# A decoder layer on one core: two more groups of unused products between the first transpositions, later landings in the planner's table, and a new order

## What is computed

```python
x = x + _L0_attn_ref(_layernorm(x, axis=-1), Wq, bq, Wk, bk, Wv, bv, Wo, bo)      # causal, with alibi bias
x = x + _L0_xattn_ref(_layernorm(x, axis=-1), ctx_2048, mask_BxS2_bk0)            # ctx is both key and value
x = x + _L0_ffn_ref(_layernorm(x, axis=-1), up_kernel, up_bias, down_kernel, down_bias)
# ffn: gelu(h @ fp4(up_kernel) + up_bias) @ fp4(down_kernel) + down_bias
# fp4: blocks of 32 rows share a power-of-two scale, codes 0, .5, 1, 1.5, 2, 3, 4, 6
```

## Time and profile before

| | us |
|---|---|
| median of 3 runs | 136.51 |
| lowest and highest | 135.77, 137.06 |
| the profiled execution | 137.31 |
| its span, first to last instruction | 135.5 |
| TensorE busy | 119.1 (88%) |
| VectorE busy | 108.1 (80%) |
| ScalarE busy | 84.3 (62%) |
| GpSimd busy | 75.5 (56%) |

### The profile page before, as it was taken

The page is one execution under the profiler, slowest core; times in us unless marked ns, Lnnn a source line. Parts: engine busy times, 40 slices in busy tenths (PEclk is TensorE's granted clock), DMA queues, the critical chain, the costliest instruction groups (busy, mean ns, idle before and its releaser), DMA issues. The chain is left out here.

```text
span 135.5 us, 3237 instructions
## 1 busy us (share of the span) xinstructions
PE 119.1 (88%) x1060; PEld 87.1 (64%) x1060; DVE 108.1 (80%) x253; ACT 84.3 (62%) x180; POOL 75.5 (56%) x140
## 2 busy tenths in 40 slices
PE   0939899999999999979999999764998989999990
PEld 0829346745557785657786766633556878999990
DVE  5382995899998799988989999969977696854632
ACT  2130479349888768856877787757568588545520
POOL 7844400145959833754661667891745979544430
PEclk9995999999999999999999999999599999999999
DMA  4999605999700000000000000000000002020112
GB/s 125 288 356 381 220 6 151 374 344 384 171 0 5 5 0 0 5 0 0 0 7 0 0 5 0 0 0 2 5 0 0 0 0 85 0 77 0 47 35 77
DMA packets 8880, 10.69 MB, mean 79 GB/s; under 512 B 1665, under 2 KB 7937, under 8 KB 8737
## 3 DMA queue, kind: packets, MB, share of 16 engines
q1 hardware_dynamic: 7776, 9.64, 21.2%
q10 hardware_dynamic: 1088, 0.86, 2.1%
HBM read 9.45 MB, written 1.05 MB: 77 GB/s over the span
## 5 line engine op out<-in xcount | busy, mean ns | idle before, releaser
L623 POOL TENSOR_TENSOR s_sb<-s_sb,s_max 128x512 f32<-128x512 f32 x16 | 16.8, 1052 | 24.9 <-DVE s_max L837 24.9
L957 DVE TENSOR_TENSOR h_lo<-h_sb,h_hi 128x256 fp32r<-128x256 f32 x32 | 15.6, 495 | 8.3 <-POOL h_hi L612 8.3
L1132 PE MATMUL bank<-xn_T,w_up_q 128*128 128x256 f16 x128 | 20.1, 291 | 1.4 <-ACT h_sb L753 1.0
L753 ACT ACTIVATE h_sb<-bank,bias_cols 128x256 f32<-128x256 f32 x32 | 14.9, 474 | 9.9 <-PE bank L1132 8.9
L612 POOL CAST h_hi<-h_sb 128x256 fp32r<-128x256 f32 x32 | 14.0, 444 | 11.7 <-ACT h_sb L753 11.7
L1148 PE MATMUL bank<-w_down_q,h_hi 128*128 128x256 f32 x64 | 18.6, 317 | 0.0
L585 POOL TENSOR_TENSOR rstd<-var_eps,minus_half 128x1 f32<-128x1 f32 x24 | 16.0, 666 | 2.0
L1148 PE MATMUL bank<-w_down_q,h_lo 128*128 128x256 f32 x64 | 16.3, 281 | 0.0
L581 POOL TENSOR_SCALAR var_eps<-mean_var 128x1 f32<-128x1 f32 x24 | 8.3, 345 | 14.4 <-DVE mean_var L786 13.6
L653 ACT ACTIVATE xn_T<-bank 128x256 f32<-128x256 f32 x16 | 6.1, 383 | 15.8 <-PE bank L990 15.6
L1003 PE MATMUL bank<-xn_T,w_T 128*128 128x512 f32 x32 | 14.6, 600 | 0.5 <-issue 0.5
(11 more groups left out here) (88 smaller groups left out, 260.8 us busy)
## 6 DMA issues: line engine op xcount, KB each, us to landing
raw_T<-in_W_up_T_dram SPq DMA_DIRECT2D x1, 1024.0 KB, 9.1
raw<-in_W_up_dram SPq DMA_DIRECT2D x1, 1024.0 KB, 11.8
raw_T<-in_W_down_T_dram SPq DMA_DIRECT2D x1, 1024.0 KB, 5.6
raw<-in_W_down_dram SPq DMA_DIRECT2D x1, 1024.0 KB, 8.1
ctx_T<-in_ctx_by_feature_dram SPq DMA_DIRECT2D x1, 1024.0 KB, 10.3
ctx_sb<-in_ctx_dram SPq DMA_DIRECT2D x1, 1024.0 KB, 13.0
out_dram<-x_sb SPq DMA_DIRECT2D x8, 128.0 KB, 1.7
x_sb<-in_x_dram SPq DMA_DIRECT2D x4, 128.0 KB, 3.9
```

What stands on the lines that cost most here:

```text
L623: pool.tensor_tensor(tile, tile, s_max[:, u % S_RING, :].unsqueeze(2).broadcast_to([P, HC, S]), ALU.subtract).then_inc(centred, 1)
L753: act.activation(h_sb[:, i % GELU_RING, :], bank[i % 2][:, 0:GN], ACT.Gelu_apprx_tanh, bias=bias_cols[:, BUP + f:BUP + f + 1], scale=1.0 / ...
L957: dve.tensor_tensor(h_lo[:, i % H_RING, :], h_sb[:, i % GELU_RING, :], h_hi[:, i % H_RING, :].bitcast(F32), ALU.subtract).then_inc(split_r ...
L1132: last = pe.matmul(dst[:, 0:GN], w_up_q[:, c, f * P:(f + 1) * P], xn_T16[:, g * GT:(g + 1) * GT, at16:at16 + P], start=(k == 0), stop=(k = ...
```

## The change

The seven unused products stay where they are. After the first transposition three more are put into TensorE's list, and after the second three more again; each transposition of the first three tiles comes after its group. In the table the third tile's landing is planned 1.1 us later and the fourth's right behind it; the loads themselves are issued as before. The planned length of the query and key weights' load is 0.2 us shorter. All weights of the planner are replaced, and so the order of every queue may be another. The banks of three stages are read from tables, with the same values as before.

```diff
-WARM = 7
+WARM = (7, 3, 3)
...
-        add("turn", (n, t), "pe", 0.22, [("norm", (n, t))] + ([("warm", ())] if n == LN1 and t == 0 else []), [ln_bank(n, t)], last)
+        add("turn", (n, t), "pe", 0.22, [("norm", (n, t))] + ([("warm", (t,))] if n == LN1 and t < len(WARM) else []), [ln_bank(n, t)], last)
...
-    loads = (("load_x", (0,), 2.1), ("load_x", (1,), 0.6), ("load_v", (), 0.5), ("load_x", (2,), 0.8),
-             ("load_x", (3,), 1.0), ("load_biases", (), 0.1), ("load_qk", (), 2.2), ("load_x", (HALF,), 0.5),
+    loads = (("load_x", (0,), 2.1), ("load_x", (1,), 0.6), ("load_v", (), 0.5), ("load_x", (2,), 1.9),
+             ("load_x", (3,), 0.1), ("load_biases", (), 0.1), ("load_qk", (), 2.0), ("load_x", (HALF,), 0.5),
...
-    add("warm", (), "pe", 1.49, [("load_x", (0,))])
+    for i in range(len(WARM)):
+        add("warm", (i,), "pe", 0.22 * WARM[i], [("turn", (LN1, i - 1))] if i else [("load_x", (0,))])
...
-        add("prob_T", (u,), "pe", 0.49, [("exp", (u,))], [2 + u % 2], ("prob_copy", (u,)))
+        add("prob_T", (u,), "pe", 0.49, [("exp", (u,))], [prob_bank(u)], ("prob_copy", (u,)))
...
 URGENCY = {
...
-    "attn_turn": 354, "quant": 142, "normalise": 100, "pv": 59, "binade": 55, "prob_T": 49, "x_table": 48,
+    "normalise": 149, "quant": 142, "x_scores": 124, "load_row_biases": 74, "v2_zero2": 51, "k_rest": 47,
...
-    "rstd": -5, "x2": -8, "scale_copy": -9, "spread_copy": -11, "x_prob_copy": -13, "q_inverse": -13,
-    "norm": -14, "v2_zero2": -15, "reload": -16, "q_step": -17, "load_qk": -18, "down": -18, "x_prob_T": -20,
...
-    "q_out": -43, "turn": -56, "scale_T": -65, "exp": -89, "x_read": -93, "v": -171,
+    "rows_copy": -38, "v": -38, "load_v": -39, "centre": -42, "rstd": -47, "x_prob_T": -49, "q_exponent": -58,
+    "x_exp": -58, "q_clip": -64, "spread_copy": -65,
...
 DRIFT = {
...
-    "binade": -6.4, "x_scale": -6.8, "norm": -7.6, "q": -8.0, "x2": -8.8, "k_rest": -9.6, "v_even": -10.4,
-    "x_prob_copy": -14.8, "q_cut": -19.2, "v_move": -24.0, "q_divide": -24.0, "scale_copy": -34.0,
-    "q_out": -36.8, "q_inverse": -140.8,
+    "v2_zero": 48.0, "scale_copy": 42.6, "binade": 40.0, "x_prob_T": 30.0, "low": 17.2, "v_copy": 12.0,
...
+    "max": -4.0, "x1": -4.4, "amax": -4.8, "load_x": -13.4, "k": -20.8, "v_move": -24.0, "q_round": -24.0,
+    "q_step": -57.6, "q_inverse": -302.4,
...
 PATIENCE = {
-    "act": 0.34, "pe": 0.12, "dve": 0.1, "pool": 0.0,
+    "pool": 0.38, "pe": 0.1, "act": 0.0, "dve": 0.0,
 }
...
                 if stage == "warm":
-                    for i in range(WARM):
+                    for i in range(WARM[at[0]]):
                         pe.matmul(bank[7][:, 0:P], ident, ident, start=True, stop=True)
...
+PROB_BANKS = (2, 3)
+UP_BANKS = ((0, 1), (0, 1), (0, 1), (0, 1))
+DOWN_BANKS = (2, 3, 2, 3)
```

More of the change, by code:

```diff
@@ L208, in stages @@
             add("split", (i,), "dve", 0.35, [("round", (i,))] + reused)
-            banks = [2 + g % 2] if f == 0 else []
+            banks = [down_bank(g)] if f == 0 else []
             add("down", (i,), "pe", 0.56, [("split", (i,)), ("q_out", (DOWN, 1))], banks, ("final", (tiles[-1],)))
@@ new lines @@
+    "prob_T": 2, "x_table": 2, "warm": 1, "q_cut": -2, "spread": -3, "q_add": -4, "q_out": -5, "load_ctx": -8,
+    "q": -10, "load_qk": -12, "add_bo": -13, "down": -13, "add_down": -15, "scale_copy": -15, "load_rows": -16,
+    "round": -19, "x_read": -19, "x_fill": -21, "load_o": -21, "q_divide": -21, "x_prob_copy": -21,
+    "store": -23, "k_flat": -25, "qk_bias": -26, "exp": -27, "load_alibi": -30, "scale_T": -33, "valid": -38,
+    "rows_copy": -38, "v": -38, "load_v": -39, "centre": -42, "rstd": -47, "x_prob_T": -49, "q_exponent": -58,
@@ L257 @@
+    "q": 4.0, "turn_copy": 3.8, "v_spread": 3.2, "x_scale": 3.2, "norm": 2.3, "spread_copy": 2.0,
+    "x_prob_copy": 1.2, "scores": 0.8, "exp": 0.2, "add": -0.4, "prob_T": -0.4, "split": -0.8, "centre": -1.2,
+    "normalise": -1.4, "attn_turn": -1.4, "x2": -1.6, "down": -2.1, "stats": -2.6, "warm": -3.3, "v_odd": -4.0,
+    "max": -4.0, "x1": -4.4, "amax": -4.8, "load_x": -13.4, "k": -20.8, "v_move": -24.0, "q_round": -24.0,
+    "q_step": -57.6, "q_inverse": -302.4,
 }
 PATIENCE = {
-    "act": 0.34, "pe": 0.12, "dve": 0.1, "pool": 0.0,
+    "pool": 0.38, "pe": 0.1, "act": 0.0, "dve": 0.0,
@@ L698, in _ @@
                         act.wait_ge(pv_ready, u - 1)
[L699 removed]
+                    act.activation(p_T[:, u % 2, :, :], bank[prob_bank(u)][:, :].rearrange("p (g q) -> p g q", g=4),
                                    ACT.Copy).then_inc(probs_copied, 1)
@@ L963, in _ @@
                     dve.wait_ge(b_down_added, t + 1)
-                    dve.tensor_tensor(x_sb[:, t, :], bank[2 + g % 2][:, (t % GT) * E:(t % GT + 1) * E],
+                    dve.tensor_tensor(x_sb[:, t, :], bank[down_bank(g)][:, (t % GT) * E:(t % GT + 1) * E],
                                       x_sb[:, t, :], ALU.add).then_inc(final_ready, 1)
@@ L1142, in _ @@
                     if f == 0:
-                        claim(2 + g % 2, (final_ready, GT * (g + 1)))
+                        claim(down_bank(g), (final_ready, GT * (g + 1)))
                     for t in range(GT):
-                        dst = bank[2 + g % 2][:, t * E:(t + 1) * E]
+                        dst = bank[down_bank(g)][:, t * E:(t + 1) * E]
                         for part, src in enumerate((h_hi, h_lo)):
@@ L1171, in qk_bank, with prob_bank, up_bank, down_bank @@
     return 5 if kind == "q" else 7
+def prob_bank(u):
+    return PROB_BANKS[u % len(PROB_BANKS)]
+def up_bank(i):
+    banks = UP_BANKS[i // FC]
+    return banks[i % len(banks)]
+def down_bank(g):
+    return DOWN_BANKS[g]
 def v_bank(h, pair):
```

30 lines of the change are left out of this document (11 added, 19 removed).

## The result

| | before | changed |
|---|---|---|
| median, us | 136.78 | 141.91 |
| lowest and highest of 4 | 135.77, 138.72 | 141.27, 143.99 |
| profiled execution, span, us | 135.5 | 140.5 |
| TensorE busy in it, us | 119.1 | 122.6 |
| VectorE busy in it, us | 108.1 | 107.8 |

The changed kernel is slower: ratio 1.0385, 95% interval 1.0285 to 1.0485. The forecast was 135.5 us, within a range of 133.2 to 138.2 us; the time lies 3.7 us above its upper end.

What follows compares the result with a forecast made beforehand. TensorE, with weak places in the opening and at 86 to 102 us, was taken as the bound. The profiled 137.31 us less 1.45 for the opening, zero for the order, less 0.4 for run differences, gave 135.5 us; range 133.2 to 138.2.

Steps and rivals of the forecast that it cites:

- What bounds the kernel: Whole span: TensorE busy 119.1 and VectorE 108.1 of 135.5 us; the down products keep TensorE busy near the end.
- the two weak places: The opening and the stretch of 86 to 102 us, each with TensorE idle time and one fall of the clock.
- (a): Opening: six more unused products, 0.9 us a group, covered by TensorE's waits of 1.20 and 0.76 us.
- (b): Opening: later planned landings let the first normalisation start at 5.90 us; keys' products at about 12.9 us, gain 1.5 us.
- The clock in the opening: With the added groups the clock stays up after 9.74 us, so the values' product takes 1.97 us, not 3.47.
- the third rival: Clock mostly holds in the opening without the groups, or VectorE gives nothing back: 136.5 us, chance 0.15.
- (c): From the opening to the last quantisation link of the second matrix: 1.2 to 1.5 us of the gain carries through.
- (d): All queues reordered by the new planner weights: effect put at zero, with 2 us to both sides.
- The fourth rival: Second matrix's quantisation ends later, its links yielding to attention's sums and maxima; two pairs give 138.2 us, chance 0.22.
- the sign of a wrong forecast: The last link of the second matrix's quantisation ending after 102.5 us; it was expected at about 100.9 us.

Runs made afterwards that it cites:

- the moved stages alone: Kernel before with first two normalisations ahead of third and fourth statistics, values' product ahead of third transposition, no added products: 135.31 us, ratio 1.0053.
- the root ahead: Changed kernel with the reciprocal root of tile 4's second layer norm ahead of one bias addition in GpSimd's list: 139.71 us, ratio 1.0208.
- root and filler: Changed kernel with tile 4's reciprocal root ahead of the bias addition and six unused products before the late transposition: 136.85 us, ratio 1.0126.
- the third experiment: Changed kernel with the planner's old urgency, drift and patience, keeping the new table and groups: 146.88 us, ratio 1.0807.
- the first experiment: Kernel before with only the new opening (two groups of unused products, moved stages), all queues behind it as before: 135.54 us, ratio 0.9941.
- the fourth experiment: Changed kernel with one product of probabilities and values put ahead of the late transposition in TensorE's list: 140.57 us, ratio 1.0318.
- The filler kernel: Changed kernel with twelve unused products right ahead of the transposition where TensorE waited 2.88 us: 139.53 us, ratio 1.0292.

## Why the prediction was wrong

- **What bounds the kernel, and the two weak places: right.** In every profile of either order the end follows the last link and the stretch of the down products behind it.
- **(a) and (b), the opening: right in its times, within 0.3 us.** 12.63 us against a forecast of 12.9, with the first normalisation at 5.88 us for 5.90. One term was mis-sized: the first group took 1.47 us, at the lower level, and not 0.9; the second 0.83. The clock column reads 1.00 there, and so did my argument for 0.9.
- **The clock in the opening: the third rival had the better of it.** With the groups the clock held, but it held without them too, in the profile of the moved stages alone. And of 59 executions of the kernel before that stand in the comparisons, 48 had a mean clock of 0.986 or more, room for at most one stretch of 3.5 us at half speed, where the profiled one had two (0.975). The rule of the Trainium skill that I cited (TensorE: Matmul & The Clock Gate, Part 1, under "What's actually happening", the free-running watch) agrees with that: the same kernel had mean clocks of 1.000, 0.987, 0.975 and 0.962. So the sum took away 1.5 us that many executions never paid; how many is open, for a mean clock doesn't tell which of the two falls was missing. The opening measured 0.6% and not 1.1%.
- **(c), the carry: right.** With the order of before the keys' products began 1.59 us earlier (12.81 us) and the last link ended 1.69 us earlier, at 100.54 us; forecast 100.9.
- **(d), the new order at zero with 2 us to both sides: this step failed.** It cost about 6 us. Two terms were missing. One is what a wait on TensorE costs when the clock falls behind it. I had the rows for it: the stretch of 86 to 98.5 us has an idle stretch and a fall behind it, and I priced such a fall at 1.7 us, but only as something that the new order might save. Here 2.88 us of waiting and 10.2 us at half speed made the last link 4.1 us later than with the root ahead (104.13 against 100.00 us) and 4.8 us later than with root and filler (99.31 us). The other is the work left behind the link. I took the stretch of the down products for fixed, "hardly stops", but what it holds depends on how much of the up products and the cross attention the order has put ahead of it: 234 or 248 records, 29.7 or 31.9 us with the clock at 1.00 in both.
- **The fourth rival: right in its place and sign, wrong in mechanism and price.** The last link did end later, beyond the 102.5 us named as the sign of a wrong forecast. But no sums and maxima had passed its links; the chain ran into a TensorE that was waiting and then slow. Its 2.7 us and the chance of 0.22 were too small, and so was the upper end of the range. An order of some 680 stages that nobody can read off the diff has no reason to be centred on zero: the third experiment's order, with the old weights and the changed table, came out 8% slower.

## What the experiments leave open

That the stall at 79 to 82 us, with the half speed behind it, and the fuller last stretch make the loss is shown. How the first splits into wait and half speed is read from single profiled executions: an execution of the changed kernel with a mean clock of 0.976, by my estimate some 7 us at half speed in place of the 13.6 of the profiled one, still took 141.27 us, only 1.0 us less. Where its half speed lay is not known. Nor was it tried to move the first up product (82.27 us) into the wait: its operands were written by 78.79 us, so it, unlike the product of probabilities and values, may have been ready work. Which of the 14 extra records of the last stretch come from which weight is not, nor why the kernel before has executions near 134.5 and near 137 us at the same mean clock.

The fastest versions are those with the order of before: with the new opening 135.54 us, 4.5% under the changed kernel's 141.91 us, and with the moved stages alone 135.31 us in another comparison. The runs don't tell these two apart, nor either from the kernel before by more than about 1%.

## What to carry to other kernels

If a planner writes the order, an edit of its table is an edit of the whole order: hold the rest of the order fixed and move only the stages that the edit is about, as the first experiment does, and judge a new order by itself. Look in a dense TensorE list for the place where it waits 2 to 3 us on a chain through three other engines: a few unused products there, or one stage moved ahead on GpSimd, were worth about 2 us each and 5 us together. Before moving "ready" work into such a wait, check the bank that it writes as well as its input: the product of the fourth experiment had its input, but not its bank. Split the end into the last gate and the work that stands behind it, and ask of every reordering what it does to each of the two.

## What the hardware showed that I had not expected

- The clock column is no witness of the first stretch. It reads 1.00 from the start, yet the records of the unused products take 0.24 us in 3.4 to 6.75 us and again in the first group (1.47 us for 6), and 0.14 us in the second group (0.83 us for 6).
- The half-speed stretch of the 2.88 us wait began 1.1 us into it, at 80.0 us, and lasted 10.2 us, though TensorE was busy in all of 82 to 90.1 us; before the change, behind a stretch with idle time, it lasted 3.5 us, and in the fourth experiment, with a wait of 3.23 us, 6.8 us. The filler kernel, with the same wait filled, had no fall there.
- GpSimd's instructions grow beside VectorE's quantisation: the bias addition 1.73 us where it takes 0.73 when alone, the root 1.01 where it takes 0.57, and the shift 0.94 where it takes 0.27, ending 0.13 us after VectorE's division. The Trainium skill (SBUF — State Buffer, "SBUF: two separate sides") says that VectorE and GpSimd share one pair of ports, that a VectorE operation with two inputs in SBUF takes part in this sharing, and that who comes second waits for the whole instruction of the first. The trace agrees for the shift: it begins inside VectorE's division (1.23 us, two such inputs) and ends just behind it.
